# A transformer block on one core: work reordered where the attention loop fills and drains, w1 loads and stores of the second input moved, output weights in fewer transfers

## The chip, the cores and the metric

The program runs on one core of one Trainium2 chip. A core has TensorE (PE, matrix products), VectorE (DVE), ScalarE (ACT), GpSimd (POOL) and SyncE (SP), which here only issues DMAs. Each engine takes its instructions in program order and waits for others on semaphores. The metric is the device time of one execution in microseconds (us), as the median of several.

## The reference

For 32 items of 100 tokens and 320 features there are three steps: self-attention, cross-attention to 361 context rows of 192 features, and a gated feed-forward layer. There are 20 heads of 16 features; all values are 32-bit floats.

```python
h1 = _ln(x, n1_g, n1_b)
x = _attn(h1, h1, q1, k1, v1, o1_w, o1_b, heads) + x      # x1, "the first input"
h2 = _ln(x, n2_g, n2_b)
x = _attn(h2, context, q2, k2, v2, o2_w, o2_b, heads) + x # x2, "the second input", an input of the last step
h3 = _ln(x, n3_g, n3_b)
a, g = jnp.split(h3 @ ff_w1 + ff_b1, 2, axis=-1)
return a * gelu(g) @ ff_w2 + ff_b2 + x
```

`_attn` projects queries, keys and values, takes a softmax of the scaled scores over each head, multiplies by the values and projects with the output weights (`o1_w`, `o2_w`).

## The kernel before

Matrix operands are split into a high and a low part (`_hi`, `_lo`, "parts"), and a product is made as several passes over them. The softmax needs a maximum: PE makes the scores once for DVE's maximum ("score"), and once more, with the maximum subtracted through extra rows of the operand stacks `qs` and `ks`, for ACT's exponential ("expin").

The program has three blocks, and at the end of each all engines meet.

1. **First stage.** For 8 groups of 4 items it makes the self-attention's queries, keys and values and stores them in DRAM (`qk_dram`, `v_dram`). PE, ACT and DVE pass tiles on; SP loads `x`, issues the stores, and loads the output weights in its queue between the stores: `head_rows` for `o1` in group 0 and for `o2` in group 5, 24 transfers of 16 rows each, so that heads lie 32 rows apart.
2. **Attention loop.** In period p four items are in work: `x = p` (cross-attention's exponentials and values), `s = p+1` (cross-attention's maxima), `c = p+2` (self-attention's exponentials, output projection, normalisation, cross-attention's queries and keys), `f = p+3` (self-attention's maxima). There are 29 periods, with a `lead_in` before them and a `run_out` after them. The order on each engine is written out by hand as calls. Tables with the same order (`FILL_*`, `DRAIN_*`, `over(...)`) give each job its turn in the three rotating work banks.
3. **Feed-forward.** Six tiles of 640 rows. The first three tiles of 128 rows are normalised and turned already in the run-out (`tile_statistics`, `normalise_tile`, `turn_tile`, `tile_high`, `tile_low`), and three pieces of the weight `ff_w1` are split there by POOL (`split_piece`).

Names that the change touches, with their lines: `load_qkv1` (self-attention's stacks of one item, nine or ten transfers), `place_kc`, `place_q2` and `place_max` (SP copies keys, queries and maxima into the stacks of cross-attention), `load_context`, `load_w1` (L641: two transfers, 393 KB, for one of ten pieces of `ff_w1`, called at the end of periods 8 to 17), `store_x2` (L582, `L586` is its transfer), `load_tiles` (L588), `head_rows` (L1839). On PE, `self_scores` (L167) and `cross_scores` (L786) fill the only pair of score banks, so each waits for DVE's maximum of the one before (L174, L1096); `scores_for_exp` is L812, `times_v` is L834, `project_out` L703 and L706, `turn_normalised` L685, `turn_q2` L722, `turn_max` L797, `project_kc` L733 to L737, `project_vc` L748 to L752. On ACT the exponential is L1419, `heads_high` L1440, `kc_high` L1388. On POOL `split_piece` is L1688 and L1690.

Each wait is on a count, as in these lines:

```python
            def result(b):
                if b > 1:
                    dve.wait_ge(x2_stored[b % 2], 16 * (b // 2))
            def store_x2(b):
                sp.wait_ge(*emptied(("O2", b, 0)))
                sp.dma_start(x2_dram[b], x2[b % 2][:]).then_inc(x2_stored[b % 2], 16)
```

## Time and profile before

| | us |
|---|---|
| median of 3 runs (lowest, highest) | 1327.53 (1322.02, 1328.48) |
| profiled execution | 1335.46 |
| its span, first to last instruction | 1333.7 |
| first stage / attention loop with its ends / feed-forward, from the start of the span | 0 to 150 / 150 to 973 / 973 to 1334 |
| busy: PE, DVE, ACT, POOL | 1248.4, 826.6, 672.8, 602.7 |

Durations and starts below are of the profiled execution, in us from the start of the span. PE is busy 94% of it, so what matters is where PE waits and where its clock is low: in the timeline a gap before an instruction stands at the row's end in brackets with what ended it, and in the table of stretches PEclk gives the granted clock of TensorE, in which 1.00 is 2.4 GHz and 0.50 is 1.2 GHz. "SPq" rows are DMA issues; their duration is the time that the issuing engine spent on them, not that of the transfer.

### The profile page before, as it was taken

The numbers are of one execution on the slowest core, as the hardware profiler recorded it, in microseconds if no ns is written. First come the engines' busy times: TensorE is split into PE (matmuls) and PEld (weight loads), VectorE is DVE, ScalarE is ACT, GpSimd is POOL, SyncE is SP. The second block draws the span as 40 slices with busy tenths as digits, with TensorE's granted clock in tenths as the row PEclk, the third lists the DMA queues.
The fourth block names the chain that finished last, engine by engine and source line by source line (L and its number), as shares of the span: only waits on it lengthen the run. The fifth ranks groups of instructions, "written<-read, shape, count | busy, mean of one in ns | idle before, by whom it ended". The sixth has DMA issues, their size and how long they took to land. (4 is left out here: it accounts for less than half of the span.)

```text
span 1333.7 us, 34303 instructions
## 1 busy us (share of the span) xinstructions
PE 1248.4 (94%) x12788; PEld 1168.4 (88%) x12788; DVE 826.6 (62%) x1606; ACT 672.8 (50%) x1622; POOL 602.7 (45%) x792
## 2 busy tenths in 40 slices
PE   6999679999999999999999999998689999999999
PEld 4899578899988898888889999987589999999999
DVE  5645458888787787777787888875445333242521
ACT  5655236666665666656666666664343232313131
POOL 5521225555555554544655555541366342333331
PEclk9999789999999999999999999998689999999999
DMA  4576644545545555445454554533011101010000
GB/s 125 192 250 231 184 144 124 157 135 149 162 129 161 162 150 181 145 140 179 135 155 142 146 164 128 171 100 87 13 55 41 45 1 50 0 49 0 25 1 25
DMA packets 105865, 154.49 MB, mean 116 GB/s; under 512 B 21500, under 2 KB 87284, under 8 KB 105716
## 3 DMA queue, kind: packets, MB, share of 16 engines
q1 hardware_dynamic: 105716, 152.49, 37.4%
q8 instruction: 95, 1.56, 0.5%
q14 instruction: 54, 0.44, 0.1%
HBM read 62.98 MB, written 28.93 MB: 69 GB/s over the span
## 5 line engine op out<-in xcount | busy, mean ns | idle before, releaser
L1419 ACT ACTIVATE probs<-expin 120x400 f32<-120x400 f32 (+2 forms) x635 | 297.4, 506 | 133.1 <-PE expin L812 130.2
L1096 DVE TENSOR_REDUCE neg_max<-score 100x2 f32<-100x722 f32 x320 | 287.7, 899 | 105.9 <-PE score L786 104.7
L812 PE MATMUL expin<-qs,ks 128*120 128x200 f32 (+2 forms) x1270 | 201.4, 273 | 1.2 <-ACT probs L1419 0.9
L786 PE MATMUL score<-ks,qs 128*100 128x362 f32 x640 | 170.3, 348 | 29.4 <-DMA qs<-q_parts 13.8
L812 PEld LDWEIGHTS expin<-qs,ks 128*120 128x120 f32 (+2 forms) x1270 | 180.4, 183 | 11.3 <-ACT probs L1419 7.8
L2654 DVE SCALAR_TENSOR_TENSOR hidden<-ps_a,b_cols,gelu 128x320 f32<-128x320 f32 x100 | 55.0, 550 | 174.2 <-PE ps_a L2578 174.1
L1610 POOL MEMSET qs<- 128x2400 f32 (+1 forms) x58 | 112.6, 1942 | 94.9 <-PE expin L812 94.9
L2816 POOL TENSOR_TENSOR hid_lo<-hidden,hid_hi 128x320 fp32r<-128x320 f32 x100 | 88.2, 882 | 121.8 <-ACT hid_hi L2724 121.6
L190 POOL TENSOR_TENSOR scaled_heads<-turned_heads,rden 128x320 f32<-128x320 f32 x63 | 48.0, 762 | 190.2 <-DVE rden L195 190.2
L786 PEld LDWEIGHTS score<-ks,qs 128*100 128x100 f32 x640 | 87.4, 168 | 50.0 <-issue 40.2
L2736 ACT ACTIVATE gelu<-ps_g,b_cols 128x320 f32<-128x320 f32 x100 | 52.8, 528 | 137.6 <-PE ps_g L2578 137.6
L834 PE MATMUL attn<-probs,vc 120*17 120x100 f32 (+1 forms) x3840 | 110.7, 255 | 0.0
L2578 PE MATMUL ps_g<-t_hi,w_hi 128*128 128x320 f32 x300 | 92.3, 313 | 9.8 <-DVEq L2493 9.8
L834 PEld LDWEIGHTS attn<-probs,vc 120*17 120x17 f32 (+1 forms) x3840 | 79.9, 99 | 19.0 <-issue 9.5
L174 DVE TENSOR_REDUCE neg_max<-score 100x10 f32<-100x1000 f32 x62 | 74.4, 1200 | 33.7 <-PE score L167 33.7
L2578 PE MATMUL ps_g<-t_hi,w_lo 128*128 128x320 f32 x300 | 91.6, 310 | 0.0
L2578 PE MATMUL ps_a<-t_hi,w_hi 128*128 128x320 f32 x300 | 91.6, 310 | 0.0
L2578 PE MATMUL ps_a<-t_hi,w_lo 128*128 128x320 f32 x300 | 91.5, 310 | 0.0
L2595 PE MATMUL ps_y<-w_hi,hid_hi 128*128 128x320 f32 x250 | 78.5, 314 | 0.0
L2596 PE MATMUL ps_y<-w_lo,hid_hi 128*128 128x320 f32 x250 | 77.1, 309 | 0.0
L2597 PE MATMUL ps_y<-w_hi,hid_lo 128*128 128x320 f32 x250 | 77.1, 308 | 0.0
L167 PE MATMUL score<-ks,qs 128*100 128x100 f32 x620 | 64.3, 252 | 7.2 <-PEq L1765 5.9
(222 smaller groups left out, 2971.0 us busy)
## 6 DMA issues: line engine op xcount, KB each, us to landing
ks<-kc_parts SPq DMA_DIRECT2D x96, 362.0 KB, 3.7
qk_dram<-qk_parts SPq DMA_DIRECT2D x32, 500.0 KB, 5.3
qs<-q_parts SPq DMA_DIRECT2D x192, 75.0 KB
ks<-qk_dram SPq DMA_DIRECT2D x96, 125.0 KB
ctx_raw<-in_ctxT SPq DMA_DIRECT2D x64, 180.5 KB
ks<-kc_parts SPq DMA_DIRECT2D x96, 90.5 KB, 2.7
qs<-qk_dram SPq DMA_DIRECT2D x64, 125.0 KB
v_dram<-v_rows SPq DMA_DIRECT2D x32, 132.8 KB
```

The lines of the kernel that those rows point to most:

```text
L174: return nc.vector.tensor_reduce(neg_max[:, :, n * i:n * (i + 1)], src, AX_X, ALU.max, negate=True)
L786: mm = pe.matmul(score[0:N, a, 0:JP], qs[2][u][:, a, q_slot(c), :], ks[2][u][:, k_slot(c), :], start=True, stop=True)
L812: mm = pe.matmul(dst, ks[a][u][:, k_slot(c) if a == 2 else c, j0:j0 + n], qs[a][u][:, :, q_slot(c) if a == 2 else c, :], start=True, stop= ...
L834: mm = pe.matmul(attn[32 * i:32 * i + D1, g * N:(g + 1) * N], v, probs[EXP_AT[a, b, g, jt] % NPT][0:n, i * N:(i + 1) * N], start=(jt == 0) ...
L1096: ins = nc.vector.tensor_reduce(dst, src, AX_X, ALU.max, negate=True)
L1419: nc.scalar.activation(probs[e % NPT][0:n, :], expin[e % 2][0:n, 0:HG * N], ACT.Exp, scale=SCALE)\
L1610: link(nc.gpsimd.memset(stack.rearrange("p a c n -> p (a c n)").bitcast(F32), 0.0))
L2578: mm = pe.matmul(bank[:, 0:W], a, b, start=(k == 0), stop=(k == len(passes) - 1))
L2595: pe.matmul(y, hid_hi[:, f, c], w2_hi[:, f, :], start=(f == 0), stop=False)
L2596: pe.matmul(y, hid_hi[:, f, c], w2_lo[:, f, :], start=False, stop=False)
L2597: mm = pe.matmul(y, hid_lo[:, f, c], w2_hi[:, f, :], start=False, stop=(f == FT - 1))
L2816: nc.gpsimd.tensor_tensor(hid_lo[:, f, c], hidden[n % 2][:], hid_hi[:, f, c].bitcast(F32), ALU.subtract).then_inc(hid_lo_made, 1)
```

## The change

Eight things change.

- `rows_of_heads` gives 12 transfers of 32 rows in place of 24 of 16 rows, for each of `o1` and `o2`. A transfer's source has an outer dimension of two.
- `load_w1` is called in the same periods, but after `place_max(2, x)` and before `load_context(f)`, not at the period's end.
- `store_x2` of the 27 items that are stored within the periods is issued by ScalarE, after `heads_high(1, c)`; SP keeps the last five.
- In the lead-in SP issues `load_qkv1(2)` first, `place_max(1, 1)` before the loads of `x` and context, and `load_qkv1(3)` earlier.
- In the lead-in PE, DVE and ACT do item 0's output projection, normalisation and query projection earlier, with the order of the other jobs fitted to it.
- In the run-out, the `cross_scores(31, i)` follow those of item 30 with item 31's values projections between them, the exponentials of item 30 come between them and after them, and the output projections of items 29 and 30 come later.
- In the run-out POOL does each `split_piece` after a `tile_deviation`, before the work on the heads of items 30 and 31.
- In the run-out DVE adds the residual of items 29, 30 and 31 (`result`) as its last three operations, and item 29's projected output is stored only then.

`clear_cross` gets a guard for items below 2, which no call here uses. The core of the diff, with the tables of numbers left out:

```diff
-    for k, f0, step in ((0, 0, 4 * DH), (2, P, 4 * DH), (1, 2 * P, 0)):
-        for i in range(HG):
-            for half in range(2):
-                f = f0 + half * step + DH * i
-                pieces.append((BLK * i + DH * half, k, w[f:f + DH]))
+    for i in range(HG):
+        r = slice(DH * i, DH * (i + 1))
+        pieces += [(BLK * i, k, w[f:f + P].rearrange("(h r) m -> h r m", h=2)[:, r]) for k, f in ((0, 0), (2, P))]
+        pieces.append((BLK * i, 1, w[2 * P:D][r].unsqueeze(0).broadcast_to([2, DH, D])))
...
             def lead_in():
+                load_qkv1(2)
                 set_key_rows()
-                load_x(1)
+                place_max(1, 1)
                 load_context(1)
-                load_x(2)
-                place_max(1, 1)
-                load_qkv1(2)
                 place_kc(0, 0)
                 place_q2(0)
+                load_x(1)
+                load_qkv1(3)
+                place_max(1, 2)
+                load_x(2)
+                place_kc(0, 2)
                 load_context(2)
-                place_kc(0, 2)
+                place_kc(1, 0)
                 load_x(3)
-                place_max(1, 2)
-                load_qkv1(3)
-                place_kc(1, 0)
 
             def run_out():
                 place_q2(30)
                 place_max(2, 29)
                 place_kc(30, 2)
-                store_x2(27)
                 place_kc(31, 0)
                 place_q2(31)
                 place_max(2, 30)
+                load_tiles()
                 place_kc(31, 2)
-                load_tiles()
+                store_x2(27)
                 store_x2(28)
...
-                y = x - 1 if x else None
-                v = y - 1 if y else None
                 place_q2(s)
                 place_max(2, x)
+                if x is not None and 8 <= x < 8 + FF // P:
+                    load_w1(x - 8)
                 load_context(f)
                 place_kc(s, 2)
                 load_x(e)
                 place_max(1, f)
                 load_qkv1(e)
-                store_x2(v)
                 place_kc(c, 0)
 
             lead_in()
             for p in PERIODS:
                 period(*roles(p), p + 4 if p + 4 < B else None)
-                if 8 <= p < 8 + FF // P:
-                    load_w1(p - 8)
...
                 self_scores(1, 0)
+                project_out(1, 0)
+                project_vc(0, 0)
                 self_scores(1, 1)
+                project_vc(0, 1)
                 turn_max(1, 1)
+                turn_normalised(0)
                 project_kc(0, 0)
                 project_kc(0, 1)
-                project_out(1, 0)
-                turn_normalised(0)
+                project_q2(0)
+                self_scores(2, 0)
+                turn_q2(0)
+                project_vc(0, 2)
...
                 project_vc(31, 2)
-                cross_scores(31, 0)
-                project_out(2, 29)
+                cross_scores(31, 3)
...
                 scores_for_exp(2, 30, 3, 2)
-                cross_scores(31, 6)
+                turn_max(2, 31)
                 scores_for_exp(2, 30, 4, 0)
-                cross_scores(31, 7)
                 scores_for_exp(2, 30, 4, 1)
                 scores_for_exp(2, 30, 4, 2)
-                times_v(2, 30, 2)
-                cross_scores(31, 8)
+                project_out(2, 29)
                 times_v(2, 30, 3)
                 times_v(2, 30, 4)
-                cross_scores(31, 9)
-                turn_max(2, 31)
-                project_out(2, 30)
                 scores_for_exp(2, 31, 0, 0)
                 scores_for_exp(2, 31, 0, 1)
                 scores_for_exp(2, 31, 0, 2)
+                turn_tile(0)
...
+                turn_tile(1)
...
                 times_v(2, 31, 3)
-                turn_tile(0)
-                turn_tile(1)
                 times_v(2, 31, 4)
                 turn_tile(2)
+                project_out(2, 30)
                 project_out(2, 31)
...
                 turn_heads(2, 29)
...
-                result(29)
...
                 maximum(2, 31, 9)
+                max_low(2, 31)
+                normalise_tile(0)
+                tile_statistics(1)
+                normalise_tile(1)
                 turn_heads(2, 30)
-                max_low(2, 31)
+                tile_statistics(2)
                 turn_back(2, 30)
-                tile_statistics(0)
-                tile_statistics(1)
-                tile_statistics(2)
-                normalise_tile(0)
-                normalise_tile(1)
-                result(30)
                 normalise_tile(2)
                 tile_low(0)
                 tile_low(1)
                 turn_heads(2, 31)
                 turn_back(2, 31)
                 tile_low(2)
+                result(29)
+                result(30)
...
+            def store_x2(b):
+                if b is None:
+                    return
+                act.wait_ge(*emptied(("O2", b, 0)))
+                act.dma_start(x2_dram[b], x2[b % 2][:]).then_inc(x2_stored[b % 2], 16)
...
+                v = y - 1 if y else None
...
                 heads_high(1, c)
+                store_x2(v)
                 kc_high(c, 1)
...
-                second_residual(31)
                 clear_cross(31)
                 scale_products(2, 29)
                 heads_low(2, 29)
+                second_residual(31)
+                pool.wait_ge(max_made, SCORE_AT[2, B - 1, HP - 1] + 1)
+                tile_deviation(0)
+                split_piece(0)
+                tile_deviation(1)
+                split_piece(1)
                 scale_products(2, 30)
+                tile_deviation(2)
+                split_piece(2)
                 heads_low(2, 30)
-                pool.wait_ge(max_made, SCORE_AT[2, B - 1, HP - 1] + 1)
-                for i in range(3):
-                    tile_deviation(i)
                 scale_products(2, 31)
                 heads_low(2, 31)
-                for i in range(EARLY):
-                    split_piece(i)
...
-                    sp.dma_start(dst[p0:p0 + DH, k, :], src).then_inc(done, 16)
+                    sp.dma_start(dst[p0:p0 + 2 * DH, k, :], src).then_inc(done, 16)
...
-                act.wait_ge(landed[f"o{a}"], 16 * 6 * HG)
+                act.wait_ge(landed[f"o{a}"], 16 * 3 * HG)
```

SP's queue in the first period with a w1 load, before. `w_raw` is the w1 load, `qs<-q_parts` is `place_q2`, `qs<-max_parts` with 24 rows `place_max(2, x)`, `ctx_raw` the context, `ks<-kc_parts` `place_kc`:

```order
L103 DMA vs_78<-v_dram 100x340
L586 DMA x_dram<-x 100x320
L550 DMA ks_0<-kc_parts 32x4x724 x3
L643 DMA w_raw<-in_ff_w 128x2x256
L644 DMA w_raw<-in_ff_w 128x1x256
L568 DMA qs_0<-q_parts 16x4x300 x6
L160 DMA qs_1<-max_parts 1x24x100 x2
L145 DMA ctx_raw<-in_ctxT 128x361
```

The same stretch of SP's queue in the changed kernel:

```order
L103 DMA vs_79<-v_dram 100x340
L549 DMA ks_1<-kc_parts 32x4x724 x3
L567 DMA qs_1<-q_parts 16x4x300 x6
L160 DMA qs_0<-max_parts 1x24x100 x2
L642 DMA w_raw<-in_ff_w 128x2x256
L643 DMA w_raw<-in_ff_w 128x1x256
L145 DMA ctx_raw<-in_ctxT 128x361
```

The store of x2 has left SP, and the w1 load stands behind the queries and the maxima, not ahead of them.

ACT's queue in the middle of a period of the changed kernel, where the store has come in (`t_hi_OT` is `heads_high`, `kc_parts` is `kc_high`, `probs` an exponential):

```order
L1384 CAST kc_parts<-work 128x362
L1415 ACTIVATE probs<-expin 121x400
L1415 ACTIVATE probs<-expin 120x400
L1436 CAST t_hi_OT<-dense_heads 128x300
L1447 DMA x_dram<-x 100x320
L1384 CAST kc_parts<-work 128x362
L1415 ACTIVATE probs<-expin 120x400
```

Before, the same rows stood without the DMA. What is now behind it on ACT is the second `kc_high` of item c and the exponentials after it.

The last rows of POOL's queue in the run-out, before (`w_hi`, `w_lo` are `split_piece`; `scaled_heads` and `t_lo_OT` are the heads of one item):

```order
L190 TENSOR_TENSOR scaled_heads<-turned_heads,rden 128x320
L1635 TENSOR_TENSOR t_lo_OT<-dense_heads,t_hi_OT 128x300
L1688 TENSOR_TENSOR w_hi_64<-w_raw,one 128x256 x3
L1690 TENSOR_TENSOR w_lo_67<-w_raw,w_hi_64 128x768
L1688 TENSOR_TENSOR w_hi_65<-w_raw,one 128x256 x3
L1690 TENSOR_TENSOR w_lo_68<-w_raw,w_hi_65 128x768
L1688 TENSOR_TENSOR w_hi_66<-w_raw,one 128x256 x3
L1690 TENSOR_TENSOR w_lo_69<-w_raw,w_hi_66 128x768
L373 UNCONDITIONAL_BRANCH
```

The same in the changed kernel, up to the last heads:

```order
L1694 TENSOR_TENSOR w_hi_65<-w_raw,one 128x256 x3
L1696 TENSOR_TENSOR w_lo_68<-w_raw,w_hi_65 128x768
L190 TENSOR_TENSOR scaled_heads<-turned_heads,rden 128x320
L1685 TENSOR_TENSOR var_eps_60<-mv_59,eps 128x1
L1686 TENSOR_TENSOR rstd_61<-var_eps_60,neg_half 128x1
L1694 TENSOR_TENSOR w_hi_66<-w_raw,one 128x256 x3
L1696 TENSOR_TENSOR w_lo_69<-w_raw,w_hi_66 128x768
L1641 TENSOR_TENSOR t_lo_OT<-dense_heads,t_hi_OT 128x300
L190 TENSOR_TENSOR scaled_heads<-turned_heads,rden 128x320
L1641 TENSOR_TENSOR t_lo_OT<-dense_heads,t_hi_OT 128x300
```

The three splits have moved from behind the last item's heads to ahead of them; the block now ends with the heads.

## Rows read from the trace of the kernel before

**Rows 1.** Stretches: length, busy (count) PE, PEld, DVE, ACT, POOL; PEclk, DMA share, GB/s.

```profile
410.23:656.66 246.43, 233.41 (x3022) 215.54 (x3021) 192.05 (x321) 151.50 (x380) 129.51 (x140) 0.99 0.52 157
656.66:867.62 210.96, 207.36 (x2721) 191.23 (x2719) 172.59 (x289) 136.28 (x342) 116.65 (x126) 1.00 0.49 148
940.71:956.99 16.28, 15.33 (x157) 11.91 (x156) 4.03 (x12) 7.83 (x17) 1.57 (x4) 0.50 0.04 11
```

**Rows 2.** Waits of PE between 210 and 890: us in total, times, longest.

```profile
PE score L786 <- DMA qs<-q_parts: 12.6, 9, 3.0
```

**Rows 3.** Timeline of SP and of PE where a w1 load is issued: start, us.

```profile
407.10 1.09 SPq L643 DMA_DIRECT2D w_raw<-in_ff_w  x1
...
413.37 1.63 SPq L160 DMA_DIRECT2D qs<-max_parts  x2
...
416.57 0.55 PE L786 MATMUL score<-ks,qs 128*100 128x362 f32 x2 [1.87 <-DMA qs<-q_parts]
```

**Rows 4.** Timeline of ACT and PE in the first stage, third group.

```profile
69.33 0.43 ACT L2291 COPY v_rows<-v_pair 100x320 f32<-100x320 f32 x1 [3.60 <-DMA v_dram<-v_rows]
...
69.81 4.13 PE L1977 MATMUL v_pair<-w_qkv,ks 128*100 128x320 f32 x16 [2.03 <-ACT v_rows L2291]
```

**Rows 5.** Timeline of SP in the first stage, from the o2 weights to the end.

```profile
105.96 12.26 SPq L1841 DMA_DIRECT2D raw<-in_o_w  x24
...
142.25 3.12 SPq L1901 DMA_DIRECT2D qk_dram<-qk_parts  x4
145.42 4.15 SPq L1856 DMA_DIRECT2D v_dram<-v_rows  x4
```

**Rows 6.** The tile w_o: duration ns min/median/max, first and last start.

```profile
L2266 ACT CAST w_o<-raw x2: 461/462/462, 88.0 to 131.1; 128x320 fp32r<-128x320 f32 x2
```

**Rows 7.** Timeline of PE in the lead-in.

```profile
150.14 1.88 PE L167 MATMUL score<-ks,qs 128*100 128x100 f32 x10 [5.93 <-PEq L1765]
...
177.86 0.54 PE L786 MATMUL score<-ks,qs 128*100 128x362 f32 x2 [1.16 <-DMA qs<-q_parts]
...
198.98 1.28 PE L167 MATMUL score<-ks,qs 128*100 128x100 f32 x10
```

**Rows 8.** Timeline of ACT, DVE and PE in one period, around the store's new place.

```profile
877.08 0.45 ACT L1440 CAST t_hi_OT<-dense_heads 128x300 fp32r<-128x300 f32 x1
877.50 0.46 ACT L1388 CAST kc_parts<-work 128x362 fp32r<-128x362 f32 x1
...
881.72 0.94 DVE L1173 TENSOR_SCALAR z<-x,mv,rstd 100x384 f32<-100x384 f32 x1 [0.21 <-POOL rstd L1607]
...
882.76 0.44 PE L685 MATMUL work<-identf,z 100*128 100x100 f32 x3
```

**Rows 9.** The tensor x_dram: issue ns min/median/max; DMA to landing.

```profile
L586 SPq DMA_DIRECT2D x_dram<-x x32: 287/340/2933, 263.3 to 964.3; - x32
...
DMA to landing us min/median/max: 2.1/2.3/3.5
```

**Rows 10.** Timeline of PE and POOL from item 31's first cross scores to the feed-forward.

```profile
916.41 0.90 PE L786 MATMUL score<-ks,qs 128*100 128x362 f32 x2 [1.21 <-issue]
...
922.75 0.58 PE L786 MATMUL score<-ks,qs 128*100 128x362 f32 x2 [0.28 <-DVE neg_max L1096]
...
924.34 0.57 PE L786 MATMUL score<-ks,qs 128*100 128x362 f32 x2 [0.60 <-DVE neg_max L1096]
...
936.25 0.25 PE L797 MATMUL work<-identf,neg_max 100*24 100x100 f32 x1 [1.10 <-DVE neg_max L1096]
...
940.71 0.97 PE L812 MATMUL expin<-qs,ks 128*120 128x200 f32 x4
...
955.79 1.20 PE L834 MATMUL attn<-probs,vc 120*17 120x100 f32 x24
...
973.43 0.61 PE L2578 MATMUL ps_g<-t_hi,w_hi 128*128 128x320 f32 x1 [9.77 <-DVEq L2493]
...
970.98 1.80 POOL L1690 TENSOR_TENSOR w_lo<-w_raw,w_hi 128x768 fp32r<-128x768 f32 x1
```

More of the change, by code:

```diff
@@ L881, in lead_in @@
                 times_v(1, 1, 4)
+                project_kc(1, 0)
+                turn_max(1, 2)
                 cross_scores(0, 0)
-                turn_max(1, 2)
                 cross_scores(0, 1)
-                project_kc(1, 0)
                 cross_scores(0, 2)
+                project_out(1, 1)
+                cross_scores(0, 3)
                 project_kc(1, 1)
-                cross_scores(0, 3)
-                project_out(1, 1)
                 cross_scores(0, 4)
@@ L898, in lead_in @@
                 cross_scores(0, 8)
-                scores_for_exp(1, 2, 0, 0)
-                cross_scores(0, 9)
                 project_vc(1, 0)
                 project_vc(1, 1)
+                cross_scores(0, 9)
+                project_kc(1, 2)
             def run_out():
                 scores_for_exp(1, 31, 1, 0)
+                turn_max(2, 29)
                 scores_for_exp(1, 31, 2, 0)
-                turn_max(2, 29)
                 project_vc(30, 2)
@@ L1007, in run_out @@
                 scores_for_exp(2, 31, 4, 2)
-                times_v(2, 31, 2)
                 times_v(2, 31, 3)
-                turn_tile(0)
-                turn_tile(1)
                 times_v(2, 31, 4)
                 turn_tile(2)
+                project_out(2, 30)
                 project_out(2, 31)
@@ L1222, in lead_in @@
                 maximum(1, 1, 0)
+                second_input(0)
+                statistics(0)
                 maximum(1, 1, 1)
+                normalise(0)
                 max_low(1, 1)
+                features_low("T2", 0)
                 kc_low(0, 0)
                 kc_low(0, 1)
-                second_input(0)
-                statistics(0)
-                normalise(0)
-                features_low("T2", 0)
-                kc_low(0, 2)
                 q2_low(0)
@@ L1250, in lead_in @@
                 maximum(2, 0, 6)
+                kc_low(1, 1)
+                maximum(2, 0, 7)
+                q2_low(1)
+                maximum(2, 0, 8)
+                maximum(2, 0, 9)
                 kc_low(1, 2)
-                maximum(2, 0, 7)
-                maximum(2, 0, 8)
-                q2_low(1)
-                maximum(2, 0, 9)
             def run_out():
@@ L1463, in lead_in @@
                 copy_product(1, 1)
+                kc_high(1, 0)
                 max_high(1, 2)
-                kc_high(1, 0)
                 heads_high(1, 1)
@@ L1468, in lead_in @@
                 features_high("T2", 1)
-                kc_high(1, 2)
                 copy_q2(1)
@@ L1472, in lead_in @@
                 q2_high(1)
+                kc_high(1, 2)
             def run_out():
-                copy_vc(30, 1)
                 copy_vc(30, 0)
@@ L1486, in run_out @@
                 exponential(2, 29, 0, 1)
+                heads_high(1, 31)
                 kc_high(31, 0)
@@ L1489, in run_out @@
                 exponential(2, 29, 1, 0)
-                heads_high(1, 31)
-                kc_high(31, 1)
                 exponential(2, 29, 1, 1)
@@ L1499, in run_out @@
                 features_high("T2", 31)
+                kc_high(31, 1)
                 exponential(2, 29, 3, 2)
-                kc_high(31, 2)
                 exponential(2, 29, 4, 0)
@@ L1504, in run_out @@
                 exponential(2, 29, 4, 1)
+                q2_high(31)
+                kc_high(31, 2)
                 exponential(2, 29, 4, 2)
-                q2_high(31)
                 copy_product(2, 29)
-                copy_vc(31, 1)
-                copy_vc(31, 0)
                 max_high(2, 30)
-                heads_high(2, 29)
-                copy_vc(31, 2)
                 exponential(2, 30, 0, 0)
@@ L1517, in run_out @@
                 exponential(2, 30, 1, 1)
+                copy_vc(31, 0)
+                copy_vc(31, 1)
+                heads_high(2, 29)
                 exponential(2, 30, 1, 2)
@@ L1528, in run_out @@
                 copy_product(2, 30)
-                max_high(2, 31)
-                heads_high(2, 30)
                 exponential(2, 31, 0, 0)
@@ L1545, in run_out @@
                 exponential(2, 31, 4, 2)
-                tile_high(0)
-                tile_high(1)
+                heads_high(2, 30)
                 copy_product(2, 31)
+                tile_high(2)
                 heads_high(2, 31)
-                tile_high(2)
             def period(x, s, c, f):
                 y = x - 1 if x else None
+                v = y - 1 if y else None
                 copy_vc(s, 1)
```

150 lines of the change are left out of this document (79 added, 71 removed).

## The prediction, made before the changed kernel ran

> **What bounds the kernel now.** I read the stretches first, then the waits, then the timeline at the seams. In the steady loop TensorE is busy and at full clock: from the start of period 19 to that of period 28, nine periods, PE is busy 207.36 of 210.96 us, 23.44 us a period [rows 1]. There only less work on PE would help, and the change takes none away. The time that can be won is where PE waits or runs at 1.2 GHz, in five places.
>
> 1. The ten periods 9 to 18 take 246.43 us where ten at 23.44 would take 234.4: 12.0 too much [rows 1]. The waits name it: PE's cross scores waited 12.6 us, nine times, for the transfers of `place_q2` [rows 2]. The timeline shows the cause: the w1 load's 393 KB are issued just ahead of `place_q2`, and the first cross scores come 1.87 us late [rows 3].
> 2. In the first stage the third group's values wait. ACT waits 3.60 us for the values' store of the group before, PE 2.03 [rows 4].
> 3. The first stage ends when SP has issued its last store, 145.42 + 4.15 = 149.57, and PE starts the next block at 150.14 [rows 5, 7].
> 4. The lead-in takes 198.98 - 150.14 = 48.8 us, more than two periods. Item 0's first cross scores come 27.7 us after its start and had waited for `place_q2` [rows 7].
> 5. In the run-out, from the last `turn_max` at 936.25, PE waits for the maxima to be placed until 940.71, does item 31's exponentials and values at clock 0.50 until 956.99, and waits at the end 9.77 us for POOL, whose splits end at 972.78 [rows 1, 10].
>
> **The change part by part,** against the profiled execution of 1335.46 us (span 1333.7). It lies 7.9 above the median of the runs, 1327.53; I subtract the same gain from both.
>
> *The w1 load behind the queries.* In its new place its packets are behind those of `place_q2` and `place_max`. Behind it stand the context, which the next period needs, the last two key tiles, which cross scores 8 need late in the period, and self-attention's stacks. Nothing changes in the bytes. If all waits go, 12.0 us are won. What is late next is `place_max(2, x)`: its issue ends at 415.00 [rows 3], and the packets of w1 can slow its landing, on which the period's first exponential waits. I take 11 won, and keep 12 and 5 as ends; 5 means 0.7 us a load kept.
>
> *Twelve transfers for 24.* For o2, 24 cost SP 12.26 us [rows 5]; twelve at the same 0.51 save 6.1, and o1's the same. At o1 SP comes earlier to the stores of the next group by 6.1, more than the 3.60 that ACT waited, so wait 2 goes. PE won it as 2.03 of waiting and as values at half clock behind it: 16 matmuls took 4.13 us, about twice what full clock needs [rows 4]. That makes 2.03 + about 1.9 = 3.9 for PE. At the stage's end SP and PE are both near: SP started the last queries' stores at 142.25, right after its queue [rows 5]. With SP 6.1 and PE 3.9 earlier, PE's results set the end: the last stores start about 5.4 earlier. I take 5, and keep 1 and 6. The output weights are cast at 88.0 and 131.1, the second 12.9 after the end of its 24 issues at 118.22, so that a slower landing of the wider pieces stays hidden [rows 5, 6].
>
> The rows show 24 pieces issued in 12.26 us and the cast 12.9 later [rows 5, 6]. The Trainium skill, "DMA: Bandwidth & Descriptors", "Rules for kernel authors", speaks against the new shape: a transfer whose outermost dimension is small runs on at most so many DMA engines, here two. With that page's 27 GiB/s an engine, an estimate for twelve pieces of 41 KB is 8.5 us on two engines, longer than the 6.1 us of their issue. By the rule a 2 us backlog would stand before the next stores; without it none. Both are under the slack, so the sum is the same by either.
>
> *The lead-in.* The chain to the first cross scores is: output projection of item 0, statistics, normalisation, turn, query projection, turn, `place_q2`. Before, two self scores with their maxima, a turn and two key projections stood ahead of it. Now only the first self scores do, so the chain starts some 7 us earlier. But SP now issues `load_qkv1(2)` first, behind a wait for the last stores of the first stage to land, and then has the rest ahead of `place_q2`: with nine transfers in 5.5, two in 1.2, two in 1.6, two in 1.7 and three in 1.9 us (an estimate from like issues, 0.5 to 0.8 each [rows 3, 5]) it gets to the queries 15 us after the block's start, and has placed them at 21 to 22, where they came at 27.7 before [rows 7]: 6 us. The ten cross scores after it are bound by the single pair of score banks, 1.59 us from one to the next [rows 10], as before. I take 6 won for the lead-in; ends are 0 and 10.
>
> *Stores on ScalarE.* 27 issues go from SP, where each took 0.34 us [rows 9]. SP is no bound in the loop, so this wins nothing. On ACT the issue stands between `heads_high` and `kc_high`, which follow each other without a gap [rows 8]. Behind `kc_high` wait DVE's low part, the next maximum, the residual, the statistics and `z`, whose turn on PE at 882.76 starts 0.10 after `z` ends at 882.66 [rows 8]. So ACT's delay reaches PE but for some tenths. If ACT dispatches the DMA while `heads_high` runs (0.45 us), the delay is nothing; if it costs all 0.34, PE loses about 0.15 a period, 4 us; at twice that, 10. I take 1 lost.
>
> On these rows SP's issue time is all that the move can save. The Trainium skill, "DMA: Bandwidth & Descriptors", "Issuing engines are not separate DMA queues", says the same of transfers from several engines: they share the same DMA engines. By a view that a second issuer brings bandwidth a gain would be due; by the rule, none, and the sum has none.
>
> *The run-out.* Cross scores of item 31 start at 916.41 [rows 10]. They wait for `place_q2(31)`, which waits for POOL's clearing after item 29's last exponential scores. These now come before cross scores 5 of item 30, some 2.2 us earlier. From there nine more at 1.59 reach the last at about 14.3 after the first, where `turn_max` came 19.8 after it before, of which 1.4 are the last scores and maximum. With one stall of 0.5 for `place_max(2, 30)`, the last maximum is ready at 914.2 + 14.3 + 0.5 + 1.4 = 930.4, 5.9 before 936.25. The exponentials of item 31 follow 4.46 later as before [rows 10]; the work kept for that gap (three expin, item 29's output projection, two of `times_v`) is near 4 us and fits. Then 16.3 us of exponentials if the clock stays at 0.50 [rows 1]. I take 6 won; the ends are 0 and 13, since at full clock PE would need half of its 15.33 us.
>
> *The end of the block.* POOL's three splits, 10.8 us, now lie beside the exponentials of item 31, ahead of heads that are not needed before the end. What is late next: after the last `times_v` (956.99 before [rows 10]) copy, turn, scaling, turn back take 3.6, the low part of tile 2 0.7, and then DVE writes items 29, 30 and 31. `result(31)` must wait until item 29's store has landed, 2.3 us after its issue [rows 9]: 3.6 + 0.8 + 0.5 + 2.4 + 0.5 = 7.8, and the store's issue 0.3. With 0.65 for the block's change that is 8.8, where 973.43 - 956.99 = 16.4 passed [rows 10]. So 7.6 go; I take 7.5, ends 5 and 8.5.
>
> Sum: -11 - 5 - 6 + 1 - 6 - 7.5 = -34.5. The profiled execution would be 1301, the median 1293.
>
> **The rivals.**
>
> *A. The store holds ScalarE up (the other side).* One SP issue of the same store took 2.933 us [rows 9]. Were that so in each period on ACT, with 0.3 absorbed, PE would lose 27 x 2.63 = 71 us: 1327.5 - 35.5 + 71 = 1363. It decides from 35.5/27 + 0.3 = 1.6 us an issue. Against it: the median is 0.34, and the long one followed six other issues.
>
> *B. The w1 load's delay only moves.* Its packets then delay the maxima as they did the queries; the gap from the maxima's issue to their use is as short. For it: the same bytes in the same periods. Against it: `place_max` is issued first. The 11 are lost: 1304.
>
> *C. The ends trade one wait for another.* `load_qkv1(2)` waits at the head of SP's queue, and `load_tiles` stands ahead of the keys that cross scores 8 need. Lead-in and run-out then win nothing but the splits' 7.5: 1327.5 - 11 - 5 + 1 - 7.5 = 1305.
>
> *D. The clock stays up.* With more work between the waits, PE does item 31's exponentials at 2.4 GHz and wins 7 more: 1286. Against it: these 16 us alternate between PE and ACT in any order.
>
> **How the numbers follow.** Forecast 0.68, B 0.10, C 0.11, D 0.06, A 0.05. The likeliest alone is 1281 to 1305. With B and C the range is 1280 to 1311; A lies outside. A change under 0.5% (6.6 us) can't be told from none here. Faster needs 1320.9 or less: all but A and a case in which B and C come together with a costly store: faster 0.91, same 0.04, slower 0.05.
>
> **What would show it.** Periods 9 to 18 take 234 to 236 us, with no wait on `qs<-q_parts`. No DMA wait before the third group's values, and the second block starts at 144 to 146. First cross scores 21 to 23 us into it, period 0 at 41 to 44. Steady periods of 23.4 to 23.6; a longer one, with PE waiting at the turn of `z`, is the store's price. POOL's splits end before item 31's heads, and PE's gap at the feed-forward's start is 2 to 3 us, with item 29's store as what ends DVE's last wait. The forecast is wrong if the periods with w1 stay above 24 us, or if a steady period grows by more than 0.3.

## The result, and the profile of the changed kernel

The changed kernel takes 1306.36 us (median of four, 1306.0 to 1307.2), the kernel before 1328.01 beside it: 21.65 us less, a ratio of 0.985 (95% interval 0.982 to 0.988). Its profiled execution took 1306.7 us with a span of 1304.9; against the 1335.46 of before that is 28.8 us less, and the sum of the prediction was made on that side. The two differences are not one number because the kernel before varies: 1322 to 1340 us over all its executions here, the changed kernel 1305.6 to 1308.5. The experiments below come back to that. One execution further down, of the kernel with its stores back on SyncE, took 1685 us at a mean granted clock of 0.655, and its median leaves it out.

Where the 28.8 us are, stage by stage (before and after from the starts of the same instructions):

| stage | before | after | difference | forecast |
|---|---|---|---|---|
| first stage, to the block's first matmul | 150.14 | 150.39 | +0.25 | -5 |
| lead-in, to period 0 | 48.84 | 46.17 | -2.67 | -6 |
| periods 0 to 27 | 668.64 | 656.86 | -11.78 | -11 and +1 |
| run-out, to item 31's last values | 89.37 | 82.74 | -6.63 | -6 |
| from there to the feed-forward | 16.44 | 8.21 | -8.23 | -7.5 |
| feed-forward | 360.27 | 360.53 | +0.26 | 0 |

The stretches after, in the columns of [rows 1]: periods 9 to 18, periods 19 to 27, item 31's exponentials and values.

```profile
407.59:642.03 234.44, 230.43 (x3023) 212.51 (x3021) 191.75 (x321) 151.06 (x380) 129.08 (x140) 1.00 0.54 163
642.03:853.42 211.39, 207.51 (x2721) 191.27 (x2719) 172.73 (x289) 136.38 (x342) 116.14 (x126) 1.00 0.49 148
925.98:936.16 10.18, 8.99 (x161) 6.93 (x158) 6.70 (x15) 8.70 (x20) 9.47 (x13) 1.00 0.01 2
```

The ten periods with a w1 load take 234.44 us, as ten others would (nine take 211.39). Item 31's exponentials and values take 10.18 us at full clock, where they took 16.28 at half [rows 1]. The waits of PE from 400 to 854 (total, times, longest) have no transfer left but a single 0.3:

```profile
PE score L782 <- DVE neg_max L174: 7.6, 19, 0.4
PE expin L808 <- DMA qs<-max_parts: 0.3, 1, 0.3
```

The first stage after, timeline of SP, DVE and PE, answers to [rows 4, 5]:

```profile
45.15 9.76 SPq L1849 DMA_DIRECT2D raw<-in_o_w  x12
54.95 2.43 SPq L1841 DMA_DIRECT2D x<-in_x  x4
...
62.72 0.49 DVE L2147 BATCH_NORM_STATS2 stats<-x 100x6 f32<-100x320 f32 x1 [3.56 <-DMA x<-in_x]
...
64.47 0.45 PE L1936 MATMUL turn_pair<-identf,z 100*128 100x100 f32 x3 [3.23 <-DVE ks L2070]
...
69.76 4.92 PE L1985 MATMUL v_pair<-w_qkv,ks 128*100 128x320 f32 x32
...
107.02 7.89 SPq L1849 DMA_DIRECT2D raw<-in_o_w  x12
...
125.84 1.64 SPq L160 DMA_DIRECT2D qs<-max_parts  x2
```

Twelve transfers took 9.76 and 7.89 us to issue, not 6.1. The third group's values run without the stop of [rows 4], but they start at 69.76 instead of 65.2: x, issued at 54.95, landed at 62.7, and PE waited 3.23 us for what is made of it. A wait went and another came. For o2, the kernel before came to the maxima at 125.26 without a pause, right behind the stores of the group; the changed kernel is done with these stores at 121.8 and then stands idle until 125.84. So the maxima set that moment, and what o2's issue saved was given back there.

The lead-in after, PE and SP, answers to [rows 7]:

```profile
150.39 1.88 PE L167 MATMUL score<-ks,qs 128*100 128x100 f32 x10 [5.43 <-PEq L1773]
...
175.02 0.64 PE L729 MATMUL work<-ctx_hi,w_c 128*128 128x362 f32 x1 [4.83 <-POOL ctx_lo L1661]
...
176.73 0.91 PE L782 MATMUL score<-ks,qs 128*100 128x362 f32 x2
...
196.56 1.06 PE L167 MATMUL score<-ks,qs 128*100 128x100 f32 x10 [0.28 <-DVE neg_max L1092]
...
162.98 0.48 SPq L145 DMA_DIRECT2D ctx_raw<-in_ctxT  x1
...
166.84 3.98 SPq L567 DMA_DIRECT2D qs<-q_parts  x6
```

The queries were issued 16.5 us into the block, 1.5 later than I expected. What came last was the split of the next context, whose load stands behind `load_qkv1(2)`.

The run-out after, PE, SP, POOL and DVE, answers to [rows 10]:

```profile
895.41 4.89 SPq L567 DMA_DIRECT2D qs<-q_parts  x6
...
901.81 0.54 PE L782 MATMUL score<-ks,qs 128*100 128x362 f32 x2 [0.56 <-DMA qs<-q_parts]
...
909.15 4.50 SPq L549 DMA_DIRECT2D ks<-kc_parts  x3
...
916.79 0.57 PE L782 MATMUL score<-ks,qs 128*100 128x362 f32 x2 [2.31 <-DMA ks<-kc_parts]
...
920.21 0.33 PE L793 MATMUL work<-identf,neg_max 100*24 100x100 f32 x1 [0.73 <-DVE neg_max L1092]
...
925.98 0.67 PE L808 MATMUL expin<-qs,ks 128*120 128x200 f32 x4
...
933.50 1.82 POOL L1696 TENSOR_TENSOR w_lo<-w_raw,w_hi 128x768 fp32r<-128x768 f32 x1
...
934.78 1.38 PE L830 MATMUL attn<-probs,vc 120*17 120x100 f32 x48
...
942.73 0.49 DVE L1154 TENSOR_TENSOR x<-work,xres 100x320 f32<-100x320 f32 x1 [1.66 <-DMA x_dram<-x]
...
944.37 0.61 PE L2586 MATMUL ps_g<-t_hi,w_hi 128*128 128x320 f32 x1 [2.72 <-DVEq L2501]
```

POOL's last split ends at 935.3, before item 31's heads, and the last thing DVE waits for is item 29's store, as forecast.

### The profile page after: what moved, and what is told of

It reads as the page before. It is cut to its first block and busy times, and to the rows that moved or that the text cites. A ratio compares the mean times of both kernels' runs of the same rounds, so it can differ in the third digit from the quotient of the medians.

```text
span 1304.9 us, 34279 instructions
## 1 busy us (share of the span) xinstructions
PE 1237.5 (95%) x12788; PEld 1157.4 (89%) x12788; DVE 829.3 (64%) x1606; ACT 672.3 (52%) x1622; POOL 602.4 (46%) x792
## 5 line engine op out<-in xcount | busy, mean ns | idle before, releaser
L808 PEld LDWEIGHTS expin<-qs,ks 128*120 128x120 f32 (+2 forms) x1270 | 177.3, 180 | 11.9 <-ACT probs L1415 8.2
L1955 PE MATMUL qk_ps<-ks,w_qkv 128*128 128x400 f32 x320 | 70.6, 365 | 1.1 <-issue 1.1
```

The lines of the kernel that those rows point to most:

```text
L808: mm = pe.matmul(dst, ks[a][u][:, k_slot(c) if a == 2 else c, j0:j0 + n], qs[a][u][:, :, q_slot(c) if a == 2 else c, :], start=True, stop= ...
```

## The experiments

Each kernel was timed beside the kernel before on the same chip; an edit is against the changed kernel unless it says otherwise.

**The w1 move alone** (edit against the kernel before).

```
 place_q2(s); place_max(2, x)
+if x is not None and 8 <= x < 8 + FF // P: load_w1(x - 8)
 load_context(f)
...
-if 8 <= p < 8 + FF // P: load_w1(p - 8)
```

> The kernel before, with the ten w1 loads moved behind place_q2 and place_max and nothing else. My theory: the move takes away the wait on the queries and makes no other, so periods 9 to 18 take 234.4 us in the profile where they took 246.4, and periods 0 to 27 take 656.9 us as in the changed kernel; both ends stay as before (period 28's start to the feed-forward's 105.8 us). A profiled execution near 1335.5 - 11.8 = 1323.7. The unprofiled runs of before lie about 7.5 below its profiled one; if the w1 wait is shorter in them, the timed gain is only 4 to 8 us (1320 to 1324), if it is the same there, 12 (1316). Rival B (the delay only moves to the maxima): no gain, 1328.

Measured: 1322.12 us against 1334.41, ratio 0.990 (0.987 to 0.993): 12.3 us. The ten periods and their waits:

```profile
PE score L786 <- DVE neg_max L174: 4.4, 11, 0.4
PE expin L812 <- ACT probs L1419: 0.4, 1, 0.4
```

No wait on the queries is left, and none on the maxima took its place: rival B is out. This kernel scatters over 4 us in six executions (1319.9 to 1324.1), before over 9.6 in eleven beside it, so the w1 wait may be a part of what varies. That is not shown: only one trace of before is kept. What the record does show is that before's time goes roughly with its mean granted clock, from 1324.5 us at 0.981 to 1340.4 at 0.968; the changed kernel has 0.982 to 0.986 throughout.

**The stores back on SyncE.**

```
 load_qkv1(e)                                          # SyncE's period
+store_x2(None if x is None or x < 2 else x - 2)
 place_kc(c, 0)
...
 heads_high(1, c)                                      # ScalarE's period
-store_x2(v)
 kc_high(c, 1)
```

> The changed kernel with the second input's stores in the loop issued by SyncE again, in their old place behind load_qkv1. My theory: a store costs ScalarE nothing in the loop and SyncE is no bound, so the periods stay at 23.44 us and the time at 1306.4, within 1 us. The prediction's own term: 1 us faster than the changed kernel (1305.4), with a period 0.04 shorter. Rival A in a mild form (0.15 a period hidden in the 23.44): 4 us faster, 1302.

Measured: 1307.25 us (median of five); periods 0 to 27 take 656.29 us for 656.86. So the stores on ScalarE cost 0.6 us in 27 or nothing, and gain nothing.

**Each store in two halves** on both engines.

```
-act.dma_start(x2_dram[b], x2[b % 2][:])
+for c in (slice(0, D // 2), slice(D // 2, D)): act.dma_start(x2_dram[b][:, c], x2[b % 2][:, c])
```

> The changed kernel with each store of the second input in two transfers of half the columns, so 54 issues on ScalarE in the loop for 27. With the stores on SyncE the 28 periods took 656.3 us, with them on ScalarE 656.7 to 657.6 in seven profiles. Theory 1 (an issue costs ScalarE next to nothing on the path): again 656.5 to 657.6, time within 1 of the changed kernel. Theory 2 (an issue costs ScalarE 0.3 or more, and one of it is hidden by slack, the second is not): periods of 23.6 to 23.8 and 4 to 9 us in all. Rival A (1.6 us and more an issue): over 40 us.

Measured: 1308.18 us, the periods 657.80. Twice the issues add some 0.9 us, at the edge of the scatter (the kernels with 27 such issues take 656.6 to 657.6). The timeline of the changed kernel's ScalarE shows why:

```profile
322.46 0.51 ACT L1415 ACTIVATE probs<-expin 121x400 f32<-121x400 f32 x1
322.85 0.29 ACTq L1447 DMA_DIRECT2D x_dram<-x  x1
322.86 0.51 ACT L1415 ACTIVATE probs<-expin 120x400 f32<-120x400 f32 x1
323.24 0.46 ACT L1436 CAST t_hi_OT<-dense_heads 128x300 fp32r<-128x300 f32 x1
323.67 0.46 ACT L1384 CAST kc_parts<-work 128x362 fp32r<-128x362 f32 x1
```

The issue (ACTq) lies wholly beside exponentials that are running. In this period it even starts 0.39 us before the cast `heads_high`, which stands ahead of it in the program, and the next instructions follow each other as closely as in [rows 8]. All 27 issues:

```profile
L1447 ACTq DMA_DIRECT2D x_dram<-x x27: 293/293/620, 252.5 to 862.5; - x27
```

The longest is 0.62 us, far under rival A's 1.6. In halves one issue took 1.75 us, so long ones do occur there too.

**24 pieces again.** `rows_of_heads` and `head_rows` as in the kernel before.

> The changed kernel with the output weights in 24 transfers each, as before. Theory 1 (the twelve wide pieces leave a backlog in front of the x loads): DVE's statistics no longer wait 3.56 us for x at 62.7, but ACT waits 3.6 us and PE 2.0 for the values' store again; the second block starts at 150.1 to 150.4, so no change in time, 1306.4 within 1. Theory 2 (the twelve pieces do help somewhere that is hidden by a slower start): it starts 1 to 3 us later and the time is 1308 to 1309.

Measured: 1308.03 us, the block starts at 150.60. (In the nine profiles of kernels whose first stage is the changed kernel's or this one's, it starts anywhere from 149.8 to 152.0, so differences under 2 us say little there.) x is no longer late (0.87), and the old wait is back:

```profile
65.13 2.58 PE L1986 MATMUL v_pair<-w_qkv,ks 128*100 128x320 f32 x16
70.31 4.01 PE L1986 MATMUL v_pair<-w_qkv,ks 128*100 128x320 f32 x16 [2.60 <-ACT v_rows L2300]
```

**x first.**

```
 if k == 0:
+    for b in range(4 * NB, 5 * NB): load_x(b)
     head_rows(raw_o[1], given["o1"], landed["o1"])
```

The same loads are left out at their old place, behind the pieces.

> The changed kernel with the four x loads of group 4 issued ahead of the twelve transfers of o1's weights, not behind them. Theory 1 (the backlog of the wide pieces holds the x loads up): x lands 2 to 2.5 us after its issue, PE's wait of 3.23 us at 64.5 and the half clock behind it go, and the third group's values start 3.5 to 4.5 us earlier, at 65 to 66. If nothing else binds, the block starts 3 to 4 earlier than 150.4 and the time is 1303; if SyncE's queue or the stores of the second-last group hold the end (SyncE starts the last o2 pieces at 107 either way and then waits for the maxima until 125.8), the gain is under 1.5 us. Theory 2 (x is late for another reason, the queries' and keys' stores behind it): x still lands 7 us after its issue and nothing changes.

Measured: 1307.28 us, the block starts at 151.44. Theory 1 holds for x, whose wait is gone, but my 3 to 4 us are not there. What now stands behind the pieces is late instead:

```profile
65.80 2.58 PE L1988 MATMUL v_pair<-w_qkv,ks 128*100 128x320 f32 x16
71.71 3.87 PE L1988 MATMUL v_pair<-w_qkv,ks 128*100 128x320 f32 x16 [3.33 <-ACT v_rows L2302]
```

**o1's pieces in three lots.**

```
 if k: store_values(k)
+if k < 3: head_rows(raw_o[1], given["o1"], landed["o1"], slice(4 * k, 4 * k + 4))
```

> The changed kernel with o1's twelve transfers in three lots of four, behind the stores of groups 0, 1 and 2, not in one lot behind group 0. Both waits were seen to trade places: with twelve in one lot PE waits 3.23 us for x, with x first or with 24 pieces it waits 2.6 to 3.3 for the values' store. Theory 1 (what stands behind one lot of wide pieces comes late, whatever it is): a lot of four holds it up by a third, which the slack covers; both waits go, the third group's values take 65 to 70.2 with no wait, and the first stage ends 3 to 4 us earlier than 150.4; time 1303. Theory 2 (SyncE's queue as a whole is the bound of the first stage from 45 on, 79.6 us being its own end): the values' store of group 2, now behind eight issues that were not there, is late in its turn; the stage ends at 149.5 to 151 and the time is 1306 to 1308.

Measured: 1302.38 us, ratio 0.976 (0.971 to 0.981). Both waits are gone, and the stage ends 3.0 us earlier than in the changed kernel, 2.4 before the earliest of those nine:

```profile
65.53 4.92 PE L1985 MATMUL v_pair<-w_qkv,ks 128*100 128x320 f32 x32
...
147.40 1.88 PE L167 MATMUL score<-ks,qs 128*100 128x100 f32 x10 [5.26 <-PEq L1773]
```

Two things changed for the values' store of group 1 here: fewer wide pieces stand ahead of it, and SP takes it up at 54.46, where it came at 60.84 in the changed kernel and 62.67 with 24 pieces. The old narrow pieces in lots of eight were not tried, so whether the wide shape has any part in the gain is open.

**The context first.**

```
 def lead_in():
+    load_context(1)
     load_qkv1(2)
...
-    load_context(1)
```

> The changed kernel with load_context(1) ahead of load_qkv1(2) in SyncE's lead-in. Theory 1 (the context behind the stacks is what made the lead-in win 2.7 where I forecast 6): the three issues fall into SyncE's wait for the stores, the context lands near 153, POOL's split ends before the key projection, PE's wait of 4.83 us at 175.0 goes, and the first cross scores come at 22 to 23 us into the block, not 26.3; the block's period 0 starts 3 to 4 us earlier: 1303. Theory 2 (place_q2(0), issued to 170.8 and landing 2 us later, sets the first cross scores): PE reaches 172.8 and waits for the queries there; the gain is 3.5 at most and the wait has a new name, qs<-q_parts. Rival: what moves into the gap is the single pair of score banks, no gain.

Measured: 1303.43 us. The wait of 4.83 is down to 1.58, and then the queries are what PE waits for, as theory 2 said: 23.0 us into the block, period 0 at 42.45 where the changed kernel has 46.17.

```profile
170.77 0.40 PE L729 MATMUL work<-ctx_hi,w_c 128*128 128x362 f32 x1 [1.58 <-POOL ctx_lo L1661]
173.04 0.55 PE L782 MATMUL score<-ks,qs 128*100 128x362 f32 x2 [1.11 <-DMA qs<-q_parts]
```

**The keys first.** In `run_out`, `place_kc(31, 2)` ahead of `load_tiles()`.

> The changed kernel with place_kc(31, 2) ahead of load_tiles in the run-out. Theory 1 (rival C's small form: the tiles' nine issues hold the keys of the last cross scores up): SyncE places the keys 4 us earlier, cross scores 8 of item 31 no longer wait 2.31 us, the last turn_max comes 2.3 earlier and with it all that follows: 1304. Theory 2 (the 2.31 lies beside DVE's maxima, which are what sets the pace): no gain, 1306. If the exponential's gap is filled less well, PE falls to half clock in item 31's exponentials again: 6 us slower, 1310 to 1312.

Measured: 1306.07 us, which is no difference in the times. In the profile there is no wait for keys, and `turn_max` comes 16.5 us after item 31's first cross scores for 18.4; the run-out is 1.7 shorter. But the wait is not a fixed one. In the ten profiles with the changed kernel's order it is 2.3 to 2.5 in four, about 0.5 in two and absent in four, so one profile without it proves little.

**The splits late.** POOL's three `split_piece` behind `heads_low(2, 31)`, the deviations left in place.

> The changed kernel with POOL's three splits of w1 behind the heads of item 31 again, the tiles' deviations left where they are. The prediction's term: the end of the block is 7.5 us later, PE waits 9.8 to 10.5 us at the feed-forward's start for POOL, 1314. If the splits beside the exponentials cost PE or ScalarE anything there, or if the feed-forward hides a part, it is less than 7.5. If it is nothing, the shorter end comes from DVE's order alone.

Measured: 1311.38 us. From the last projection to the feed-forward it takes 12.2 us for 4.2 (936.68 to 948.86), and PE's gap is the old one:

```profile
936.68 0.95 PE L699 MATMUL work<-w_o,t_hi_OT 128*100 128x320 f32 x5 [2.33 <-ACT t_hi_OT L1436]
...
948.86 0.60 PE L2585 MATMUL ps_g<-t_hi,w_hi 128*128 128x320 f32 x1 [10.68 <-DVEq L2500]
```

That is 7.9 lost there, while the time is only 4 to 5 longer. Beside the exponentials POOL's splits had cost PE 1.0 in most profiles (a wait for a normalised tile, which is gone here); the exponentials and values ran at full clock in this profile (10.1 us); and the feed-forward is 0.3 to 0.9 shorter. That the splits end behind the heads costs what I said; that it is all lost in the time was too simple.

**An empty gap.** PE's `project_out(2, 29)` moved from ahead of item 31's exponentials to behind `turn_tile(2)`.

> The changed kernel with item 29's output projection (eight matmuls, 2.9 us in the profile at 922.0) moved from the gap ahead of item 31's exponentials to behind them. Theory 1 (that projection fills the gap, and a filled gap keeps the clock: rival D's mechanism): the gap is as long, PE idles 1.5 to 2.5 us in it and is at 1.2 GHz for most of item 31's exponentials, which take 13 to 16 us, not 10.2; the feed-forward starts 4 to 7 later: 1311 to 1313. Theory 2 (the clock was kept up by what ran before the gap, and the projection only fills it): the exponentials start up to 1 earlier, at full clock, the projection's 1.5 lies in the waits at the end, and the time is 1305 to 1307.

Measured: 1309.64 us. PE was at half clock in the gap, and back at full clock in the exponentials (columns as in [rows 1]):

```profile
920.72:924.83 4.11, 3.92 (x55) 3.18 (x55) 3.30 (x8) 1.64 (x4) 3.95 (x6) 0.50 0.02 5
924.83:935.27 10.44, 9.29 (x161) 7.22 (x158) 7.68 (x16) 8.21 (x19) 10.13 (x14) 0.97 0.01 2
```

So the projection itself is not needed for the clock. But theory 1 is not out, because the gap did not stay as long as it assumed: it closed from 5.77 to 4.11 us, and PE was busy for 3.92 of them. Whether a gap with PE idle costs the clock was not tested. The run-out is 2 to 3 us longer (93.07 for 90.95 and 90.11): the exponentials start at most 1.7 earlier, and the projection is done at the end. Under the kernel before's order the same stretch ran at half clock in a second profile too, that of the w1 move alone:

```profile
928.54:944.81 16.27, 15.32 (x157) 11.91 (x156) 3.38 (x10) 7.81 (x17) 0.97 (x3) 0.50 0.04 10
```

In both profiles the old order has PE idle for 2.67 us before a projection and then alternates with ScalarE at 0.19 us waits. The new order is better, but not as good as the first profile of the changed kernel has it. The same kernel profiled again (next run):

```profile
920.29:924.10 3.81, 3.43 (x63) 2.84 (x64) 3.08 (x8) 1.62 (x4) 3.65 (x6) 1.00 0.02 5
924.10:936.50 12.40, 10.34 (x160) 8.05 (x156) 8.26 (x16) 8.59 (x20) 11.55 (x15) 0.86 0.01 2
```

Here the gap ran at full clock and a part of the exponentials at half, behind a wait of 1.0 us for a normalised tile (the runs x first and three lots have the same wait, and no half clock behind it). Over the twelve profiles with the new order, the exponentials and values of item 31 take 10.1 to 13.8 us at granted clocks of 1.00 to 0.75, for 16.3 at 0.50 in both with the old. Gap and exponentials together take 13.9 to 17.7 us, for 20.7 and 21.4. Which part of the new order lifts the clock was not found.

**The changed kernel again, and three edits together** (lots of four, context first, keys first), side by side on one chip.

> The changed kernel once more, to have its time beside the next three on one chip. The kernel before took 1334.4 to 1334.5 us beside my first eight runs and 1328 beside the first measurement of the change; the changed kernel 1306.4 there. Theory 1 (what differs from run to run is the w1 wait of the kernel before, which the change takes away): the changed kernel takes 1305 to 1308 here too, while before is anywhere from 1322 to 1339. Theory 2 (the chips differ as a whole): it lies as far above 1306.4 as before lies above 1328.

> The changed kernel with the three edits together: o1's weights in three lots of four, load_context(1) first in the lead-in, place_kc(31, 2) ahead of load_tiles. By themselves they moved the block's start by 3.0 us, period 0 by 3.7 from the block's start, and the run-out by 1.7. If they add up, 8.4 off 1306.4: 1298, with the first cross scores 22.5 to 23 us into the block and the feed-forward at 936. If the earlier context splits or the maxima take part of it back: 1300 to 1301.

Measured: the changed kernel 1307.15 us beside 1336.6 for before, ratio 0.979 (0.976 to 0.982); theory 1 holds, it takes the same time beside a slower kernel before. The three edits: 1298.2, ratio 0.972 (0.969 to 0.975), 9.0 us less than the changed kernel and the fastest of all. The marks of its profile:

```profile
144.77 1.88 PE L167 MATMUL score<-ks,qs 128*100 128x100 f32 x10 [4.46 <-PEq L1773]
...
188.93 1.06 PE L167 MATMUL score<-ks,qs 128*100 128x100 f32 x10 [0.27 <-DVE neg_max L1092]
...
845.97 1.00 PE L167 MATMUL score<-ks,qs 128*100 128x100 f32 x10
...
934.85 0.61 PE L2586 MATMUL ps_g<-t_hi,w_hi 128*128 128x320 f32 x1 [2.43 <-DVEq L2501]
```

Against the changed kernel beside it the block starts 6.2 earlier, the lead-in is 2.4 and the run-out 1.2 shorter. In the medians the three edits add up well: 4.8, 3.7 and 1.1 less than the changed kernel alone, 9.0 together. The profiles add up less well. The first stage is the same program as in the run with three lots, which ended it at 147.40, not 144.77, so some 2.6 of the 6.2 are what varies between executions. The first cross scores come 25.2 into the block, later than I expected: PE waits 2.28 us for the stacks first, 0.54 with the context first alone.

## Why the prediction was right, and where it was not

The forecast of the median was 1293 and 1306.36 was measured: inside the whole range of 1280 to 1311, but just above its likeliest part, 1281 to 1305. By the number alone, rivals B (1304) and C (1305) were nearer. Only the table by stage and the experiments tell that B did not happen and C only in small parts.

*The w1 load* was right in place, cause and size: 11.8 in the profile, 12.3 timed alone.

*The first stage* is the step that failed, and the term that was mis-sized: 5 forecast, nothing measured. Two of its numbers were wrong. "Twelve at the same 0.51" took an issue to cost the same whatever it carries; an issue took 0.60 us in the median and 0.81 or 0.66 on average. And the backlog that I priced at 2 us and called "under the slack" held x up: it was there 7.8 us after SP took up the load (54.95 to 62.72), 2.3 before. I had looked for the slack of the stores behind the pieces, and the x loads stand ahead of them with only about 2 us to spare. The view of the transfers shows it: DMA engines busy in tenths, then GB/s, over 8.9 us in 40 slices. First before, while the 24 pieces were issued, then the changed kernel, up to the end of x's issue.

```profile
DMA  2614242332233343312030203030202120311211
GB/s 74 129 36 129 57 114 66 91 80 85 85 94 85 79 90 78 69 58 69 17 63 23 81 0 92 0 75 17 81 12 75 17 63 23 58 41 40 52 46 40
...
DMA  2111111111111111111111111111131111155666
GB/s 99 54 45 54 45 45 54 36 54 47 41 50 52 46 46 46 46 52 46 46 52 46 46 46 46 46 46 46 52 120 52 46 46 46 46 109 196 224 242 230
```

Before, the rate swings between 0 and 129 GB/s: some slices are all but empty, so nothing piles up. After, it is a digit of 1 and 46 GB/s, steadily, with no empty slice. At that rate 41 KB take 0.89 us, close to the 0.81 of an issue, as if SP went at the pace of the few engines that the pieces use, and twelve would take 10.7, an estimate from this rate. The Trainium skill, "DMA: Bandwidth & Descriptors", "Rules for kernel authors", has a transfer confined to at most as many engines as its outermost dimension counts, here two. The trace agrees by its steady rate; the digit alone (two of sixteen are 0.125, which prints as 1) would not do, since before has digits of 1 too. The same page's bandwidth gave an estimate of 8.5 us for twelve pieces, and their issue took 9.76 and 7.89: the rule that I set aside as changing nothing was the better price. Four orders show that it is the lump that costs, wide or narrow: with it whole, either x or the values' store is late by some 3 us; in three lots neither is, and the stage ends at 147.4 and 144.8. So most of the 3.9 us that I gave PE were there to be had, but not with the lump in one place.

*The lead-in* was half right. The queries' time was right within 1.5 us, and the rest of the step, that they are what comes last, was not: the context's split was. With it out of the way the lead-in is 6.4 shorter than before in one profile, my 6, and 4.7 in the other, with the three edits. I had counted what stands ahead of `place_q2` and not what the key projection ahead of the cross scores waits for.

*The stores* were right in kind. The 1 us was a bound too high, at most 0.6 was seen, and rival A never came near. The two prices of an issue did not go together: 0.15 for 0.34 takes 0.19 as hidden, rival A 0.3; neither was needed.

*Up to item 31's values* the total was right by luck, by two errors that cancel. The last `turn_max` came 1.8 us earlier, not 5.9: the first cross scores gained 0.4 instead of 2.2 (`place_q2(31)` was taken up 1.6 earlier in the run-out, at 895.41, but its six issues took 4.89 us where they had taken 3.75, and `turn_max(2, 30)` stands ahead of the scores now), and `load_tiles` ahead of the keys cost 2.3, a small part of rival C. The gap to the exponentials grew by 1.3, PE being at 0.55 of its clock in it. Against that, rival D happened in this profile: the exponentials ran at full clock, 6.1 us. In the others it happened in whole or in part, 6.2 down to 2.4 us. I gave it 0.06 because "these 16 us alternate between PE and ACT in any order"; that sentence was wrong, and it was not tested by anything in the trace of before.

*The end of the block* was right: 8.2 for 7.5, and with the splits put back 7.9 of it are lost again.

Forecast 34.5 and measured 28.8 in the profile thus differ by the first stage (5.3) and the lead-in (3.3), less 2.9 in the rest. In the medians the gain was 21.65 in the first comparison and 29.4 in the last: the profile that I read the terms from was a slow one of before, 8 above its median, and I subtracted all of them from the median too. That the change removes just the part that varies would fit, but is not shown.

## What to carry to other kernels

Fewer, wider transfers are not cheaper when each keeps to a few DMA engines: look at their GB/s while they are issued, and at what stands behind them in the queue with the least slack; dealing them out in small lots won here what merging them did not. Where a chain is shortened, list everything that the instruction at its end waits for, also through the instructions ahead of it on its engine, since the second-last often sets the time. Take a gain that is read off one profile of a varying kernel from the range of its times, not from that one.

## What the runs showed of the hardware

An issue of a transfer on ScalarE's queue lay beside its running activations (0.29 us beside 0.51), ahead of the cast before it in the program, and all 27 cost at most 0.6 us; I had taken that for the best of three cases. Twelve transfers with an outermost dimension of two ran at a steady 46 GB/s, and a load issued behind them was there after 7.8 us, not 2.3. TensorE ran 16.3 us at granted clock 0.50 although it was busy 15.3 of them, in both profiles of one order of the instructions. With another order the same work took 10.1 to 13.8 us at 1.00 to 0.75 in twelve profiles, and where a half-clock stretch fell, before item 31's exponentials or within them, differed between two profiles of one kernel.
